# Routing moved from behind the last sum into it: pages opened tile by tile, rows scattered at once

## The chip, the cores and the metric

The kernel runs on one core of one Trainium2 chip. The time is the device time of that core in microseconds (us), the median of several runs. The profile is one further execution with the hardware profiler.

## The reference

Four graph layers over 3125 nodes of 256 features and 50000 edges, each added to its input and layer-normalised. The last one holds the part that matters here, a top-2 mixture of experts:

```python
x = gc + (feats @ W_res + b_res)
logits = x @ Wg + bg                      # 64 experts
vals, idx = jax.lax.top_k(logits, 2)
gates = jax.nn.softmax(vals, axis=-1)
order = jnp.argsort(e_flat)               # rows grouped by expert, at most 1024 each
h1 = gelu(einsum('ecd,edh->ech', buf, w1) + b1);  h2 = einsum('ech,ehd->ecd', h1, w2) + b2
out = zeros.at[tok_s].add(g_s[:, None] * y_s)
y = x + out;  batch norm over the nodes
```

What counts is that each node's row goes to its two experts and comes back; in which place of an expert's buffer a row stands doesn't matter.

## The kernel before

The 3125 rows are T = 25 tiles of 128. The sum over edges is made as a product with a dense 3200 x 3200 matrix of edge counts, built in the first stages and kept in DRAM; it is applied seven times (stages l0, l1, h1a, h1b, h2a, h2b, l3). In each, TensorE goes through 25 tiles; a tile's sum is 25 matmuls of 128x512 (line 1044), its matrix block loaded by SyncE. Between these matmuls `aggregate` puts side steps for earlier tiles, every fourth matmul (`gap`), in the order of its list. Every engine has its own stream of instructions, in an order written out by `pipeline`: in turn n a stage with lag g works on tile n - g, and an engine takes its stages strictly in the order of the list. Semaphores join the engines. `Steps.done` makes the next instruction wait for the one before.

In l3 the side steps are: transpose of Xn (lag 1, line 1082, needs POOL's `l3_own`, line 1750), transpose of the sum G (lag 1), transpose of V (lag 2), the two dense products (lag 1), the logits (lag 2, line 1098). VectorE: `l3_sum` (lag 1, line 1494), `l3_x4` (lag 2, line 1631), `l3_top` (lag 3: bias, maximum, index, two copies, lines 1636 to 1642). POOL: `l3_own` copies the tile's own rows to Xn (lag 1), `l3_keep` copies V to X4 (lag 2, line 1755).

Behind l3 comes the stage "route". VectorE (`dve_moe`) makes one-hot rows for all tiles at once, a running count over the tiles (line 600), and TensorE ranks the rows (lines 482 to 485). From the counts come each expert's pages of 128 rows, in the experts' order (lines 605 to 614), the table `etab` of the expert of each page, and each row's slot (lines 627 to 641). SyncE then loads the weights of the first four pages (lines 421, 425); POOL scatters the rows in 50 indirect DMAs of 128 rows (line 731) into `expert_rows_in` and waits for them. All engines meet at `phase_end`.

In the stage "experts" each page takes a turn: SyncE loads rows, w1, w2 and b2 (a ring of four), TensorE transposes the rows (line 494) and makes both products (lines 502, 512), POOL stores the result (line 741). In "combine" POOL gathers each row's two results (line 750), VectorE weighs and adds them and normalises.

## Time and profile before

| | |
|---|---|
| median of 3 runs | 2228.75 us (2226.08 to 2236.04) |
| profiled execution | 2222.63 us, its span 2221.0 us |
| TensorE (PE) busy | 1861.6 us, 84% |
| VectorE (DVE) busy | 829.7 us, 37% |
| ScalarE (ACT) busy | 469.3 us, 21% |
| GpSimd (POOL) busy | 348.8 us, 16% |
| stage l3 | about 1414 to 1636 us |
| stage route | 1636 to 1736 us |
| stage experts | 1736 to about 2071 us |

The times of the rows count from the span's start. A busy time is the sum of an engine's instructions; a row of the timeline has in brackets the engine's idle time before it and what ended that. PE is a matmul, PEld the load of its weights, SPq a DMA issued by SyncE. The granted clock is TensorE's, as a share of 2.4 GHz.

### The profile page before, as it was taken

To read this page: it belongs to the slowest core of one execution; us is meant where nothing else is said; L and a number is where in the kernel's file an instruction comes from. 1 tells how busy PE (TensorE), PEld (TensorE's weight loads), DVE (VectorE), ACT (ScalarE), POOL (GpSimd) and SP (SyncE) were. 2 spreads that over 40 slices of the span, in tenths; PEclk is the share of its full clock that TensorE was granted. 3 is DMA by queue.
4 is the path that set the end of the run, shared out by engine and by line. 5 is a ranking of instruction groups with operands and counts; after the bars stand their busy time and mean duration, and the time that the engine had idled before them with its cause. 6 is when DMAs were issued, how large, how long until landed. Compare 5 with 4: busy or idle time off the path is not lost. (4 is left out here: it accounts for less than half of the span.)

```text
span 2221.0 us, 32876 instructions
## 1 busy us (share of the span) xinstructions
PE 1861.6 (84%) x9113; PEld 1473.7 (66%) x9115; DVE 829.7 (37%) x2415; ACT 469.3 (21%) x1245; POOL 348.8 (16%) x573
## 2 busy tenths in 40 slices
PE   1888989799899899999999999899940699999441
PEld 0355656588688688777778788688830688888320
DVE  4865554444434411122211177412151122222256
ACT  0033344322223211111111111111110223223010
POOL 1011222311111100000000022100007111111361
PEclk8566555899999999999999999999975799999656
DMA  4167888999688688766678888788823699999521
GB/s 118 30 237 260 279 290 301 341 319 320 214 278 265 196 272 290 251 214 213 216 240 286 277 288 290 250 289 275 279 67 125 214 368 373 372 373 374 186 78 58
DMA packets 284883, 553.32 MB, mean 249 GB/s; under 512 B 17170, under 2 KB 208328, under 8 KB 281608
## 3 DMA queue, kind: packets, MB, share of 16 engines
q1 hardware_dynamic: 275976, 528.36, 71.2%
q0 software_dynamic: 8832, 24.13, 3.2%
q8 instruction: 27, 0.44, 0.1%
q14 instruction: 48, 0.39, 0.1%
HBM read 415.14 MB, written 137.29 MB: 249 GB/s over the span
## 5 line engine op out<-in xcount | busy, mean ns | idle before, releaser
L1044 PE MATMUL psum<-xsa,blk 128*128 128x512 f32 x2500 | 637.6, 405 | 14.6 <-DVEq L342 8.2
L1044 PEld LDWEIGHTS psum<-xsa,blk 128*128 128x128 f32 x2500 | 463.8, 191 | 107.0 <-DVEq L342 8.7
L1044 PE MATMUL psum<-xsb,blk 128*128 128x512 f32 (+1 forms) x1875 | 416.6, 369 | 5.9 <-DVEq L342 5.9
L1044 PEld LDWEIGHTS psum<-xsb,blk 128*128 128x128 f32 x1875 | 322.2, 190 | 64.4 <-issue 7.2
L1386 DVE TENSOR_SCALAR onehots<-counts_scratch 128x348 bf16<-128x348 f16 x464 | 161.5, 374 | 119.3 <-PE psum L949 75.1
L949 PE MATMUL psum<-onehots 128*128 128x349 bf16 x464 | 166.8, 466 | 40.9 <-DVE onehots L1391 39.7
L502 PE MATMUL psum<-route,expert_weights 128*128 128x128 f32 x1360 | 169.8, 279 | 0.0
L502 PEld LDWEIGHTS psum<-route,expert_weights 128*128 128x128 f32 x1360 | 160.3, 194 | 1.2
L512 PE MATMUL psum<-expert_weights,route 128*128 128x256 f32 x672 | 159.1, 380 | 0.2 <-ACT route L561 0.2
L949 PEld LDWEIGHTS psum<-onehots 128*128 128x128 bf16 x464 | 51.9, 112 | 146.5 <-DVE onehots L1386 116.1
L1730 POOL TENSOR_SCALAR ve<-mv 128x1 f32<-128x1 f32 x75 | 16.8, 223 | 822.2 <-DVE mv L1501 822.2
L561 ACT ACTIVATE route<-psum,b1T 128x128 f32<-128x128 f32 x340 | 96.9, 368 | 229.1 <-PE psum L502 229.1
L968 PE MATMUL psum<-identR,band_rows 128*128 128x130 f32 x625 | 139.3, 405 | 6.1 <-ACT blk L1163 5.3
L968 PEld LDWEIGHTS psum<-identR,band_rows 128*128 128x128 f32 x625 | 132.2, 319 | 9.8 <-ACT blk L1163 5.5
L669 DVE TENSOR_TENSOR route<-psum,route 128x256 f32<-128x256 f32 x84 | 35.7, 425 | 257.9 <-PE psum L512 257.9
L512 PEld LDWEIGHTS psum<-expert_weights,route 128*128 128x128 f32 x672 | 121.3, 190 | 13.4 <-ACT route L561 0.4
L494 PE MATMUL psum<-identF,route 128*128 128x128 f32 x172 | 35.7, 290 | 86.8 <-DMA route<-expert_rows_in 86.3
L1494 DVE SCALAR_TENSOR_TENSOR G<-psum,binv,Lo 128x256 f32<-128x256 f32 x50 | 24.2, 484 | 219.8 <-ACT Lo L1215 219.8
L1222 ACT ACTIVATE tT<-psum 128x256 f32<-128x256 f32 x175 | 67.1, 384 | 171.7 <-PE psum L1082 170.2
L741 POOL DMA_DIRECT2D expert_rows_out<-route x84 | 45.4, 541 | 298.4 <-DVE route L669 298.4
L494 PEld LDWEIGHTS psum<-identF,route 128*128 128x128 f32 x172 | 18.3, 143 | 110.0 <-DMA route<-expert_rows_in 92.5
L1494 DVE SCALAR_TENSOR_TENSOR G<-psum,ndst,Lo 128x256 f32<-128x256 f32 x50 | 24.2, 484 | 179.0 <-ACT Lo L1215 176.7
(292 smaller groups left out, 1859.5 us busy)
## 6 DMA issues: line engine op xcount, KB each, us to landing
blk<-counts_src_on_rows SPq DMA_DIRECT2D x125, 832.0 KB, 4.6
blk<-counts_src_on_rows SPq DMA_DIRECT2D x125, 768.0 KB, 4.4
expert_weights<-in_L_gnn_w SPq DMA_DIRECT2D x176, 512.0 KB, 6.2
blk<-counts_dst_on_rows SPq DMA_DIRECT2D x50, 832.0 KB, 4.5
counts_dst_on_rows<-band_rows SPq DMA_DIRECT2D x25, 1600.0 KB, 7.2
blk<-counts_dst_on_rows SPq DMA_DIRECT2D x50, 768.0 KB, 4.3
counts_src_on_rows<-blk SPq DMA_DIRECT2D x13, 1600.0 KB, 8.1
counts_src_on_rows<-rblk SPq DMA_DIRECT2D x12, 1600.0 KB, 8.6
```

The source lines that it names most:

```text
L494: mm = e.transpose(psum[:, par, k * P:(k + 1) * P], xin[n][:, k * P:(k + 1) * P], identF[:, :])
L502: mm = e.matmul(psum[:, 2 + par, h * P:(h + 1) * P], w1s[n][:, k, h * P:(h + 1) * P], xTs[par][:, k * P:(k + 1) * P], start=(k == 0), stop ...
L512: mm = e.matmul(psum[:, 4 + par, 0:F], hTs[par][:, h, :], w2s[n][:, h, :], start=(h == 0), stop=(h == HT - 1))
L561: mm = e.activation(hTs[par][:, h, :], psum[:, 2 + par, h * P:(h + 1) * P], ACT.Gelu, bias=b1T[:, h, bass.ds(ex, 1)])
L669: e.tensor_tensor(yout[n], psum[:, 4 + par, 0:F], b2s[n], ALU.add)\
L741: e.dma_start(ybuf[bass.ds(c * P, P), :], yout[n]).then_inc(S(f"rows_stored{n}"), 16)
L949: e.matmul(o, one_d[:, u, :], one_s[:, u, 0:FW + 1], start=False, stop=True, skip_group_check=True).then_inc(S("onehots_used"), 1)
L968: mm = e.matmul(psum[:, s + k // 3, o:o + TURNED], band_rows[par][:, t * P:(t + 1) * P], identR[:, :], start=True, stop=True)
L1044: mm = e.matmul(o, blk[n][:, k * P:(k + 1) * P], XS[:, k, :, 0:Fw], start=(k == 0), stop=(k == T - 1 and not own))
L1222: e.activation(o, pick(a, par), func, **kw).then_inc(S("tile_" + sig), 1)
L1386: e.tensor_scalar(one_s[:, u, 0:FW], iota_f, scol[:, bass.ds(c, 1)], wcol[:, bass.ds(c, 1)], ALU.is_equal, ALU.mult).then_inc(S("sources_r ...
L1494: e.scalar_tensor_tensor((G if o is None else o)[:, 0:w], agg[par][:, 0:w], tcol(scale, i), Lo[:, 0:w], ALU.mult, ALU.add).then_inc(S("til ...
```

## The change

The route stage's work is put into l3, tile by tile. `l3_top` also makes the tile's one-hot rows `picks` and their sum `chosen`. TensorE has a new side step, `ranks` (lag 4, third in the list): two matmuls give each row's rank within the tile and the tile's count for each expert. VectorE has a new stage `l3_slots` (lag 4), which keeps for each expert the room left in its open page, the place where that ends, and the number of pages opened; where a tile's rows pass the room, it opens the next free page. From this come the slots of the tile's rows (`slot_to`, line 1656 of the changed kernel). POOL has a new stage `l3_scatter` (lag 4): it waits for the slots, issues the tile's two scatters (line 1782), and adds the opened pages to `page_expert` (line 1786). Its own copy is now line 1770 and keep line 1775. Pages thus stand in the order in which they are opened, not in the experts' order; `dve_moe` only makes the table from `page_expert`. The deepest lag of l3 is 4 instead of 2 on TensorE and 3 on VectorE. Both logits buffers become one (`logits_read`), since bank 7 of PSUM holds the ranks.

```diff
@@ -473,17 +483,6 @@
...
-            e.wait_ge(S("running_counts"), 1)
-            tpb = BANK // NE
...
-            e.matmul(psum[:, 4, 0:NE], onesB[:, :], before_tile[:, T, :], start=True, stop=True)\
-                .then_inc(S("ranked"), 1)
...
@@ -583,64 +582,19 @@
         def dve_moe(e):
             phase_end(e, "l3")
             st = Steps(e, S("dve_route"))
-            e.tensor_tensor(gap, top_val[:, :, 1], top_val[:, :, 0], ALU.subtract).then_inc(S("top_gap"), 1)
-            st.done(e.tensor_copy(idxf, top_idx[:, :, 0:TOP]))
-            one_hot = (OH1, OH2)
...
-            st.done(e.tensor_tensor(chosen, OH1, OH2, ALU.add))
...
-            for t in range(T):
-                st.done(e.tensor_tensor(before_tile[:, t + 1, :], before_tile[:, t, :], chosen[:, t, :], ALU.add))
-            e.sem_inc(S("running_counts"), 1)
-            e.wait_ge(S("ranked"), 1)
...
+            e.wait_ge(S("pages_noted"), T)
+            st.done(e.tensor_tensor(page_expert, page_expert, iota_e[:, :], ALU.mult))
+            e.tensor_reduce(ecol[:, 0:1], page_expert, AX.X, ALU.add).then_inc(S("chunk_experts"), 1)
+            st.done(e.tensor_scalar(eint[0:1, 0:1], pages[0:1, 0:1], float(RING - 1), None, ALU.add))
             st.done(e.tensor_scalar(nturn[0:1, 0:1], eint[0:1, 0:1], RING.bit_length() - 1, None,
...
             e.wait_ge(S("chunk_experts_up"), 1)
             st.done(e.tensor_copy(etab[0:1, :], psum[0:1, 6, 0:P]))
             e.sem_inc(S("experts_known"), 1)
-            first_row = ebase.unsqueeze(1).to_broadcast([P, T, NE])
-            for k in range(TOP):
-                st.done(e.tensor_tensor(M, one_hot[k], ranks, ALU.mult))
...
-                st.done(e.scalar_tensor_tensor(keep[:, k, :], rk[:, k, :], float(CAP), valid[:, :],
-                                               ALU.is_lt, ALU.mult))
-                st.done(e.tensor_tensor(slot[:, k, :], slot[:, k, :], keep[:, k, :], ALU.mult))
-                st.done(e.tensor_copy(slot_from[:, k, :], slot[:, k, :]))
-                st.done(e.tensor_scalar(rk[:, k, :], keep[:, k, :], -1.0, 1.0, ALU.mult, ALU.add))
-                st.done(e.tensor_tensor(rk[:, k, :], rk[:, k, :], trash[:, k, :], ALU.mult))
-                st.done(e.tensor_tensor(slot[:, k, :], slot[:, k, :], rk[:, k, :], ALU.add))
-                st.done(e.tensor_copy(slot_to[:, k, :], slot[:, k, :]))
-                e.sem_inc(S("slots_ready"), 1)
+            e.tensor_tensor(gap, top_val[:, :, 1], top_val[:, :, 0], ALU.subtract).then_inc(S("top_gap"), 1)
+            st.done(e.tensor_scalar(keep, slot, 0.0, None, ALU.is_ge))
+            st.done(e.tensor_scalar(slot_from[:, :, :], slot, 0.0, None, ALU.max))
...
@@ -724,12 +678,6 @@
         def pool_moe(e):
             phase_end(e, "l3")
-            for k in range(TOP):
-                e.wait_ge(S("slots_ready"), k + 1)
-                for t in range(T):
-                    e.indirect_dma_start(out=xbuf, out_offset=bass.IndirectOffsetOnAxis(ap=slot_to[:, k, t:t + 1], axis=0),
-                                         in_=X4[:, t, :], in_offset=None).then_inc(S("rows_scattered"), 16)
...
@@ -1094,6 +1042,8 @@
+                    if sig == "logits" and not (isinstance(i, int) and i == 0):
+                        e.wait_ge(S("logits_read"), i)
@@ -1101,6 +1051,14 @@
...
+            def ranks(i, par):
+                e.wait_ge(S("picks_made"), i + 1)
+                e.wait_ge(S("ranks_read"), i + 1)
+                e.matmul(psum[:, 7, 0:NE], triB[:, :], chosen[par], start=True, stop=True)
+                e.matmul(psum[:, 7, NE:2 * NE], onesB[:, :], chosen[par], start=True, stop=True)\
+                    .then_inc(S("picks_ranked"), 1)
...
@@ -1123,9 +1081,10 @@
             aggregate("l3", XSa, F, False, [
                 (1, turn("l3", "own_copied", "x_turned", pT2, Xn, KF)),
                 (1, turn("l3", "sum_read", "g_turned", pT, G, KF)),
+                (4, ranks),
                 (2, turn("l3", "x4_made", "x4_turned", px4, V, KF)),
                 (1, dense("l3", ["xT", "gT"], "pre", pD[0], two(tT, wgc) + two(tT2, wrs))),
-                (2, dense("l3", ["x4T"], "logits", [o[:, 0:NE] for o in pD2], two(tT3, wgt)))])
+                (2, dense("l3", ["x4T"], "logits", pD2[0][:, 0:NE], two(tT3, wgt)))])
...
@@ -1619,7 +1578,17 @@
...
-            st4 = Steps(e, S("steps_l3"), 3)
+            st4 = Steps(e, S("steps_l3"), 4)
+            e.memset(rooms[:, 0, :], 0.0)
+            e.memset(rooms[:, 1, :], float(CAP))
+            e.memset(ends_at, 0.0)
+            e.memset(pages, 0.0)
+            st.done(e.memset(page_expert, 0.0))
+            st.done(e.tensor_scalar(page_first, pcol[:, 0:1], float(P), None, ALU.mult))
+            st.done(e.tensor_scalar(beyond, valid[:, T - 1:T], -1.0, FALL, ALU.add, ALU.mult))
+            e.sem_inc(S("pages_set"), 1)
+            e.sem_inc(S("ranks_read"), 1)
...
@@ -1632,16 +1601,67 @@
             def l3_top(i, par):
                 st4.tile(i)
+                if i >= 2:
+                    e.wait_ge(S("picks_ranked"), i - 1)
                 e.wait_ge(S("tile_logits"), past("l3", "logits") + i + 1)
-                st4.done(e.tensor_tensor(U[:, 0:NE], pD2[par][:, 0:NE], bgb[:, :], ALU.add))
+                e.tensor_tensor(U[:, 0:NE], pD2[0][:, 0:NE], bgb[:, :], ALU.add).then_inc(S("logits_read"), 1)
+                e.wait_ge(S("logits_read"), i + 1)
...
                 e.tensor_copy(row(top_val, i), max8[:, 0:TOP])
-                e.tensor_copy(row(top_idx, i), idx8[:, 0:TOP]).then_inc(S("tile_top"), 1)
-                e.wait_ge(S("tile_top"), past("l3", "top") + i + 1)
-            pipeline(e, [(1, l3_sum), (2, l3_x4), (3, l3_top)], unrolled=True)
+                st4.done(e.tensor_copy(top_idx[:, 0:TOP], idx8[:, 0:TOP]))
+                st4.done(e.tensor_tensor(picks[par], iota_e[:, :].unsqueeze(1).to_broadcast([P, TOP, NE]),
+                                         top_idx[:, 0:TOP].unsqueeze(2).to_broadcast([P, TOP, NE]), ALU.is_equal))
+                if i == T - 1:
+                    e.tensor_scalar(picks[par], picks[par], valid[:, T - 1:T], None, ALU.mult).then_inc(S("picks_valid"), 1)
+                    e.wait_ge(S("picks_valid"), 1)
+                e.tensor_tensor(chosen[par], picks[par][:, 0, :], picks[par][:, 1, :], ALU.add).then_inc(S("picks_made"), 1)
+            room, left = rooms[:, 0, :], rooms[:, 1, :]
+            st5 = Steps(e, S("steps_pages"), 19)
+            def l3_slots(i, par):
+                st5.tile(i)
+                e.wait_ge(S("picks_ranked"), i + 1)
+                if i >= 2:
+                    e.wait_ge(S("pages_noted"), i - 1)
+                rank, many = psum[:, 7, 0:NE], psum[:, 7, NE:2 * NE]
+                pair = [P, TOP, NE]
+                st5.done(e.tensor_tensor(taken, many, left, ALU.min))
+                st5.done(e.tensor_tensor(past_room, rank.unsqueeze(1).to_broadcast(pair), rooms, ALU.is_ge))
+                e.tensor_tensor(rows_of, rank, room, ALU.subtract).then_inc(S("ranks_read"), 1)
+                st5.done(e.tensor_tensor(new, taken, room, ALU.is_gt))
+                st5.done(e.tensor_tensor_scan(so_far, ones[:, 0:NE], new, 0.0, ALU.mult, ALU.add))
+                st5.done(e.tensor_tensor(first, so_far, new, ALU.subtract))
+                st5.done(e.tensor_scalar(first, first, pages[:, 0:1], float(P), ALU.add, ALU.mult))
+                st5.done(e.tensor_tensor(further, first, ends_at, ALU.subtract))
+                st5.done(e.tensor_tensor(past_room[:, 0, :], past_room[:, 0, :], further, ALU.mult))
+                e.wait_ge(S("ranks_read"), i + 2)
+                st5.done(e.tensor_tensor(rows_of, rows_of, ends_at, ALU.add))
+                st5.done(e.tensor_tensor(rows_of, rows_of, past_room[:, 0, :], ALU.add))
+                st5.done(e.scalar_tensor_tensor(rows_of, past_room[:, 1, :], -FALL, rows_of, ALU.mult, ALU.add))
+                st5.done(e.tensor_tensor(picked, picks[par], rows_of.unsqueeze(1).to_broadcast(pair), ALU.mult))
+                st5.done(e.tensor_reduce(slot[:, :, i], picked, AX.X, ALU.add))
+                if i == T - 1:
+                    e.tensor_scalar(slot[:, :, i], slot[:, :, i], beyond, None, ALU.add).then_inc(S("picks_valid"), 1)
+                    e.wait_ge(S("picks_valid"), 2)
+                st5.done(e.scalar_tensor_tensor(above, slot[:, :, i], 0.0, trash[:, :, i], ALU.is_lt, ALU.mult))
+                e.tensor_tensor(slot_to[:, :, i], slot[:, :, i], above, ALU.max).then_inc(S("slots_ready"), 1)
+                st5.done(e.scalar_tensor_tensor(further, further, float(P), new, ALU.add, ALU.mult))
+                st5.done(e.tensor_tensor(ends_at, ends_at, further, ALU.add))
+                st5.done(e.tensor_tensor(rooms, rooms, taken.unsqueeze(1).to_broadcast(pair), ALU.subtract))
+                st5.done(e.scalar_tensor_tensor(room, new, float(P), room, ALU.mult, ALU.add))
+                e.scalar_tensor_tensor(of_page[par], first, page_first, new, ALU.is_equal, ALU.mult)                    .then_inc(S("pages_opened"), 1)
+                st5.done(e.tensor_tensor(pages, pages, so_far[:, NE - 1:NE], ALU.add))
+                e.wait_ge(S("slots_ready"), i + 1)
+            pipeline(e, [(1, l3_sum), (2, l3_x4), (3, l3_top), (4, l3_slots)], unrolled=True)
...
@@ -1754,7 +1774,19 @@
...
-            pipeline(e, [(1, l3_own), (2, l3_keep)], unrolled=True)
+            def l3_scatter(i, par):
+                e.wait_ge(S("slots_ready"), i + 1)
+                e.wait_ge(S("tile_x4_kept"), past("l3", "x4_kept") + i + 1)
+                for k in range(TOP):
+                    e.indirect_dma_start(out=xbuf, out_offset=bass.IndirectOffsetOnAxis(ap=slot_to[:, k, i:i + 1], axis=0),
+                                         in_=X4[:, i, :], in_offset=None).then_inc(S("rows_scattered"), 16)
+                e.wait_ge(S("pages_opened"), i + 1)
+                e.tensor_tensor(page_expert, page_expert, of_page[par], ALU.add).then_inc(S("pages_noted"), 1)
+                e.wait_ge(S("pages_noted"), i + 1)
+            e.wait_ge(S("pages_set"), 1)
+            pipeline(e, [(1, l3_own), (2, l3_keep), (4, l3_scatter)], unrolled=True)
...
```

On TensorE, one turn of l3's loop, before. `identF,Xn` and `identF,G` are the transposes of lag 1, `identF,V` that of lag 2:

```order
L1082 MATMUL psum<-identF,Xn 128x128 [waits tile_own_copied]
L1082 MATMUL psum<-identF,Xn 128x128
L1044 MATMUL psum<-xsa,blk 128x512 x4
L1079 REGISTER_ALU
L1082 MATMUL psum<-identF,G 128x128 [waits tile_sum_read]
L1082 MATMUL psum<-identF,G 128x128
L1044 MATMUL psum<-xsa,blk 128x512 x4
L1082 MATMUL psum<-identF,V 128x128 [waits tile_x4_made]
```

and in the changed kernel:

```order
L1030 MATMUL psum<-identF,Xn 128x128 [waits tile_own_copied]
L1030 MATMUL psum<-identF,Xn 128x128
L992 MATMUL psum<-xsa,blk 128x512 x4
L1030 MATMUL psum<-identF,G 128x128 [waits tile_sum_read]
L1030 MATMUL psum<-identF,G 128x128
L992 MATMUL psum<-xsa,blk 128x512 x4
L1059 MATMUL psum<-route,triB 128x64 [waits ranks_read,picks_made]
L1060 MATMUL psum<-route,onesB 128x64
L992 MATMUL psum<-xsa,blk 128x512
L992 MATMUL psum<-xsa,blk 128x512 [waits block_in01]
L992 MATMUL psum<-xsa,blk 128x512 x2
L1030 MATMUL psum<-identF,V 128x128 [waits tile_x4_made]
```

The ranks stand behind the two transposes of lag 1, and what came there before is four matmuls later.

On POOL, two turns of l3 before:

```order
L1750 COPY Xn<-X 128x256 [waits tile_x_turned]
L1755 COPY X<-V 128x256 [waits tile_x4_made]
L1750 COPY Xn<-X 128x256 [waits tile_x_turned]
L1755 COPY X<-V 128x256 [waits tile_x4_made]
L1750 COPY Xn<-X 128x256 [waits tile_x_turned]
```

and one in the changed kernel, with the copies on either side:

```order
L1775 COPY X<-V 128x256 [waits tile_x4_made]
L1782 DMA expert_rows_in<-X,slot_to 21248x256 [waits tile_x4_kept,slots_ready]
L1782 DMA expert_rows_in<-X,slot_to 21248x256
L1786 TENSOR_TENSOR route<-route 128x64 [waits pages_opened]
L1770 COPY Xn<-X 128x256 [waits tile_x_turned,pages_noted]
L1775 COPY X<-V 128x256 [waits tile_x4_made]
```

The scatters and the note stand between one tile's keep and the next tile's own copy.

## Rows read from the trace of the kernel before

**Rows 1.** Windows by stage (busy us, clock, DMA share, GB/s): l3, experts' stage.

```profile
core 0: us, PE busy (x) PEld busy (x) DVE busy (x) ACT busy (x) POOL busy (x), PEclk, DMA share, GB/s
...
1440.00:1628.00 188.00, 188.00 (x942) 156.95 (x941) 39.63 (x176) 35.37 (x87) 16.36 (x44) 1.00 0.77 258
...
1745.00:2080.00 335.00, 323.15 (x2172) 285.69 (x2171) 66.62 (x167) 96.56 (x340) 45.42 (x84) 0.99 1.04 361
```

**Rows 2.** Timeline (start us, duration us), PEld, one turn of l3.

```profile
1586.24 0.37 PEld L1082 LDWEIGHTS psum<-identF,Xn 128*128 128x128 f32 x2
...
1588.54 0.37 PEld L1082 LDWEIGHTS psum<-identF,V 128*128 128x128 f32 x2
...
1594.84 0.37 PEld L1082 LDWEIGHTS psum<-identF,Xn 128*128 128x128 f32 x2
```

**Rows 3.** Timeline of the same turn, VectorE and POOL.

```profile
1586.33 0.48 DVE L1494 SCALAR_TENSOR_TENSOR G<-psum,ndst,Lo 128x256 f32<-128x256 f32 x1 [6.44 <-ACT Lo L1215]
...
1586.85 0.42 DVE L1631 TENSOR_TENSOR V<-psum,bc_gc 128x256 f32<-128x256 f32 x1
...
1587.34 0.40 POOL L1755 COPY X<-V 128x256 f32<-128x256 f32 x1 [7.86 <-DVE V L1631]
...
1587.68 0.40 POOL L1750 COPY Xn<-X 128x256 f32<-128x256 f32 x1
...
1588.33 0.16 DVE L1642 COPY route<-idx 128x2 uint32<-128x2 uint32 x1
```

**Rows 4.** Timeline, VectorE's 64-column instructions behind l3.

```profile
1652.84 0.29 DVE L609 TENSOR_TENSOR_SCAN route<-ones,route 128x64 f32<-128x64 f32 x1
1653.16 0.23 DVE L610 TENSOR_TENSOR route<-route 128x64 f32<-128x64 f32 x1
1653.43 0.26 DVE L612 TENSOR_SCALAR route<-route,pcol 128x64 f32<-128x64 f32 x1
1653.72 0.22 DVE L613 TENSOR_REDUCE route<-route 128x1 f32<-128x64 f32 x1
1653.97 0.15 DVE L614 TENSOR_SCALAR route<-route 128x1 f32<-128x1 f32 x1
```

**Rows 5.** Timeline, from the last sum to the first expert matmul.

```profile
1628.78 0.47 ACT L1215 ACTIVATE Lo<-psum,ndst 128x256 f32<-128x256 f32 x1 [4.79 <-PE psum L1044]
...
1655.75 0.41 SPq L421 DMA_DIRECT2D expert_weights<-in_L_gnn_w  x1
...
1663.99 0.18 DVE L641 CAST slot_to<-route 128x25 uint32<-128x25 f32 x1
...
1665.21 1.26 POOL L731 DMA_INDIRECT expert_rows_in<-X,slot_to  x1 [31.35 <-DVEq L642]
...
1727.94 0.96 POOL L731 DMA_INDIRECT expert_rows_in<-X,slot_to  x1 [0.30 <-issue]
...
1736.52 0.69 PE L494 MATMUL psum<-identF,route 128*128 128x128 f32 x2 [82.06 <-DMA route<-expert_rows_in]
```

**Rows 6.** Windows as in rows 1, while the first weights load.

```profile
1667.00:1669.00 2.00, 0.00 (x0) 0.00 (x0) 1.97 (x2) 0.00 (x0) 1.70 (x2) 0.50 1.07 368
1669.00:1671.00 2.00, 0.00 (x0) 0.00 (x0) 1.97 (x2) 0.00 (x0) 1.43 (x2) 0.50 0.67 245
```

**Rows 7.** Timeline, TensorE's waits in h1b and at its end.

```profile
1090.72 0.44 PE L1082 MATMUL psum<-identF,G 128*128 128x128 f32 x2 [0.58 <-DVE G L1518]
...
1113.62 0.44 PE L1082 MATMUL psum<-identF,G 128*128 128x128 f32 x2 [2.40 <-DVE G L1518]
```

**Rows 8.** Windows as in rows 1, behind h1b's end.

```profile
1115.90:1119.30 3.40, 2.37 (x6) 1.96 (x7) 0.42 (x1) 0.18 (x1) 0.00 (x0) 0.51 0.00 0
```

**Rows 9.** Timeline, a gather beside a long add in the combine stage.

```profile
2100.74 1.48 DVE L683 TENSOR_TENSOR X<-X,bc_bet 128x1280 f32<-128x1280 f32 x1
2100.83 2.22 POOL L750 DMA_INDIRECT expert_weights<-expert_rows_out,slot_from  x1 [0.30 <-issue]
```

**Rows 10.** Line 750's gathers: ns min/median/max.

```profile
L750 POOL DMA_INDIRECT expert_weights<-expert_rows_out,slot_from x50: 942/946/2260, 2085.7 to 2152.3; - x50
```

69 lines of the change are left out of this document (24 added, 45 removed).

## Prediction

> **What bounds the kernel now.** I read the stage windows first [rows 1]. In l3, the last of the seven sums, TensorE is busy for all of the 188 us looked at, at full clock, and the DMA engines for 0.77; in the experts' stage it is busy for 323 of 335 us. So both are TensorE's. Between them lies a stretch in which TensorE does next to nothing, read from the timeline [rows 5]: the last tile's sum is being read at 1628.78, and the first expert matmul starts at 1736.52. Those 107.7 us are what the change is after. Most of them is POOL: 50 indirect scatters, the first at 1665.21, the last at 1727.94, thus 1.27 us apart, of which 0.96 is the instruction and 0.30 the step to the next.
>
> One turn of l3 is the other thing to see. TensorE's transpose of Xn starts at 1586.24 and the next turn's at 1594.84: a turn is 8.60 us [rows 2]. On DVE it holds 2.16 us of work (1586.33 to 1588.49), on POOL 0.74 us [rows 3]. All the rest of their time is free.
>
> **What goes.** The scatters between the stages, VectorE's 25 running counts and its 128x1600 passes over all tiles, and nine ranking matmuls. What is left between the last sum and the first expert matmul has to be built up anew.
>
> **What is added per turn.** *TensorE*: two bf16 matmuls of 64 columns (lines 1059 and 1060 of the changed kernel), with their loads. Two f32 loads for a transpose took 0.37 us [rows 2]; these are smaller and cost between nothing and that. I take 0.25, so TensorE's own turn becomes 8.85. *VectorE*: two more instructions in `l3_top` (0.5), and 22 in `l3_slots`. A dependent instruction of 64 columns follows the one before by 0.27, a scan by 0.32 and a reduction by 0.25 [rows 4]; for 128 columns I take 0.34, between 64 columns (0.23 long) and 256 (0.48 long) [rows 3, 4]. Up to `slot_to` there are sixteen: ten of 64 columns (one doesn't wait) 2.5, three of 128 columns 1.0, the scan 0.32, two of 2 columns 0.4: 4.2 us. The six behind it, which POOL's scatter doesn't need, cost 1.4. VectorE's turn is 2.16 + 0.5 + 5.6 = 8.3 us, just inside 8.85. Alone it would hide, with 0.5 us to spare. *POOL*: two scatters and a 128x64 add, some 3 us; alone it would hide as well. *DMA*: 256 KB more per turn, at a share of 0.77 [rows 1]; I cost it at nothing, hidden by the free share; without that cover it is 0.7 us a turn at the 361 GB/s of the experts' stage.
>
> **What they are worth in a ring.** They are not alone, since POOL takes its steps in one order: own copy, keep, then the wait for the slots, the scatters, the note. The next tile's own copy (Xn) is queued behind that wait, and TensorE's transpose waits for that copy, three matmuls into its turn. The slots wait for the ranks, which TensorE makes behind the two transposes of the same turn. So one turn's transpose depends on the last one's through three engines:
> - transpose of Xn to ranks made: from 1586.24 to 1588.54, where the transpose of V stands now, is 2.30 [rows 2]; with the ranks and the pipeline's end 2.85;
> - slots up to `slot_to`: 4.2, and 0.05 for the semaphore;
> - `slot_to` to the first scatter: 1664.17 to 1665.21 is 1.04, the semaphore's own instruction included [rows 5]. POOL's plain copy of V starts at 1587.34, 0.07 after the instruction that made V ends at 1587.27 [rows 3]. These are the two bounds; I take 0.9, since it is the same instruction;
> - two scatters, 0.96 + 0.30 + 0.96 [rows 5], with 0.1 for meeting VectorE: 2.3;
> - the add for the page's expert, between nothing and the 0.40 of a 256-column copy [rows 3], and a step to it and a wait for itself: 0.5;
> - the own copy 0.40 [rows 3] and the semaphores: 0.5.
>
> The sum is **11.3 us**, against a TensorE turn of 8.85: TensorE stands for 2.45 us in each turn ahead of its transpose. What is queued behind is the whole sum of that tile. The first scatter is in turn 4, so 20 turns grow by 11.3 - 8.6 = 2.7 us: **+54 us**. With every bound at its low end (0.07 for the start, nothing for the add) the ring is 10.1, with the high ones 11.6.
>
> **The clock in it.** In h1b TensorE waits 0.58 us in every turn and keeps full clock. At that stage's end it waited 2.40 us, and the next stage began at a granted 0.51, that is the 1.2 GHz level, for 3.4 us [rows 7, 8]. A wait of 2.45 in every turn is of the second kind. 3.4 us at half clock lose 1.7 us of matmul time, and as they begin near the end of the wait they fall upon the transposes and ranks, which are part of the ring. Bounds: nothing in any turn, or 1.7 in all 20, 34 us. I take 1.35 in two turns of three, about 0.9 on average: **+18 us**. The Trainium skill, "TensorE: Matmul & The Clock Gate", Part 1, says that "the default state is throttled, and activity releases the throttle"; by that a ring which leaves TensorE idle pays twice, and by the opposite view, a clock that only a long stop takes away, the sum below would be 18 us lower. The two rows of this trace lean to the first.
>
> **The tail.** From the last tile's sum (1628.78 now) the new order runs: VectorE starts 0.6 later, but the ranks it needs stand behind the own copy that still waits for POOL; slots of tile 21 from 4.0 to 9.7; then turns of 7.9 and 7.5 us to 25.1, as each still has tops and slots; the last `slot_to` at 29.8; scatters and note to 33.5. Nothing of this is under the sum, since the slots lag four tiles. Then 0.25 for the stage's end, two instructions on the page table, 0.5, and from the experts' column (ended at 1654.12) to SyncE's first weight load (1655.75) 1.63 as now [rows 4, 5]: 35.9. The 4 MB of the eight first loads kept the DMA engines full until about 1670, 14.3 us after that issue [rows 6]. These loads were covered by the scatters and now lie open: the first rows are issued behind them. With 0.6 for rows and start, the first expert matmul comes at **50.8 us** in place of 107.7: **-57 us**. The experts' stage then starts with the same full ring of weights, so I let it and everything behind it unchanged, the number of pages too: a page is opened when an expert's room is used up, as many as a count rounded up gives.
>
> **Sum.** -57 + 54 + 18 = +15 us, on the profiled execution's 2222.63: 2237.6. The median of the runs shown is 6.1 us over that execution, so I forecast **2244 us**, 0.7% slower. About 0.5%, 11 us, is what a measurement of this kernel tells from no change.
>
> **The rivals.**
> 1. *The ring holds, the clock doesn't fall.* For it: TensorE is still busy nearly 80% of a turn, far more than in the stretch behind the last sum. Against it: the row at h1b's end. Then -57 + 54 = -3 us: 2226, no change. Chance 0.25.
> 2. *Faster: the ring is shorter.* Its place is the start of the scatter behind its wait: the 1.04 us of the trace may be the cost of a queue that had been idle for 31 us. If POOL reaches the wait with the instruction prepared, and the add is cheap, the ring is 10.4 or less; TensorE then waits 1.5 us or less, the clock stays, and l3 gains 36 us: -21, 2208. The point that decides is a ring of 11.2 without clock loss, or about 10.8 with some. At its far end the ring falls under VectorE's 8.85 and the gain is -50. Chance 0.2, nearly all near -21.
> 3. *The ring is longer: POOL and VectorE hold each other up.* In the combine stage a scatter's sister, the gather of line 750, took 2.22 us in place of 0.95 beside VectorE's 1.48 us add of two SBUF operands [rows 9]. Here VectorE's two-operand instructions are 0.23 us each, and six to ten of them fall beside the scatters, the note and the own copy. If each of POOL's four waits out one or two, the ring is 12.3, and with the clock 13.5: -57 + 74 + 24 = +41, 2270. Against it: the 50 gathers have a median of 0.946 us [rows 10], though two instructions of 0.48 us run beside each pair. Chance 0.1. The Trainium skill, "SBUF — State Buffer", calls the pair of ports that VectorE and GpSimd share "an exclusive lock, not a bandwidth split", held for the whole of a VectorE instruction with two SBUF inputs against a GpSimd one that reads SBUF. By that rule this is the case to expect, though with short instructions a small one; the row of 2.22 agrees with it.
>
> **How the numbers follow.** The forecast case has 0.45: ring 11 to 11.6, clock lost in a part of the turns, +4 to +30 us. Slower by over 0.5%: most of that, 0.38, and rival 3: 0.48. Within 0.5%: rival 1 and the lower edge of the forecast: 0.27. Faster: rival 2 and what rival 1 gives below -11: 0.25. The likeliest case's own range is 2233 to 2259. The range is 2202 to 2276: down to rival 2 with a few us under it, up to rival 3; outside lies a ring that doesn't bind, and one over 12.5.
>
> **What will show it.** In the timeline of the changed l3 the transposes of Xn should stand 11 to 13 us apart from the fifth turn on and 8.6 before; TensorE's largest wait there should be on POOL's copy at line 1770, 2 us and more each, not on VectorE's sum. `slot_to` should be followed by the first scatter 0.9 us later. The granted clock of l3, now 1.00, should fall to 0.8 to 0.95. From the last sum to the first expert matmul should be 51 us, with the DMA engines full for about 14 of them and no POOL scatter behind the first 34. I am wrong if the turn stays under 10 us (the ring doesn't bind: some 50 us faster), if TensorE waits for VectorE instead (its turn is over 9), or if the tail is over 60 us.

## The result, and the profile after

| | before | changed |
|---|---|---|
| median, same chip | 2228.31 us (4 runs, 2226.08 to 2236.04) | 2202.60 us (4 runs, 2201.74 to 2204.00) |
| ratio, 95% interval | | 0.9888 [0.9871, 0.9906] |
| profiled execution | 2222.63 us, span 2221.0 | 2202.93 us, span 2201.2 |

The change makes the kernel 1.1% faster. The forecast was 0.7% slower, so the sign is wrong; 2202.6 lies at the very edge of the range. It is the case of rival 2: a ring shorter than 10.4 us, full clock. Between the profiled executions the change is 19.7 us, between the medians 25.7; the median before lies 5.7 us over its profiled execution, and the changed kernel's 0.3 under.

The windows of the changed kernel, as in [rows 1], for l3 ahead of the fourth turn, l3 with the scatters in it, the tail with its two halves, and the experts' stage:

```profile
core 0: us, PE busy (x) PEld busy (x) DVE busy (x) ACT busy (x) POOL busy (x), PEclk, DMA share, GB/s
1440.00:1455.00 15.00, 15.00 (x76) 12.21 (x76) 6.33 (x28) 3.26 (x8) 1.15 (x3) 1.00 0.83 271
1455.00:1640.00 185.00, 162.57 (x815) 128.16 (x815) 131.07 (x580) 29.30 (x72) 55.05 (x90) 1.00 0.82 261
1663.00:1700.00 37.00, 6.90 (x34) 5.14 (x34) 26.41 (x120) 1.79 (x5) 11.79 (x18) 0.60 0.10 36
1700.00:1718.00 18.00, 0.91 (x5) 0.50 (x5) 2.34 (x13) 0.49 (x2) 0.00 (x0) 0.50 0.84 277
1735.00:2050.00 315.00, 310.49 (x2100) 276.15 (x2100) 64.41 (x162) 91.70 (x321) 43.91 (x81) 1.00 1.07 369
```

TensorE was busy for 188.00 of 188.00 us of l3 before. Now it stands for 22.4 of 185, while its granted clock stays at 1.00. Who holds it is one row of TensorE's waits from 1440 to 1663 us (total us, times, longest):

```profile
PE psum L1030 <- POOL Xn L1770: 24.9, 20, 1.5
```

That is the own copy, in 20 turns, as the ring would have it, but 1.24 us each and not 2.45. One turn in the timeline, all engines:

```profile
1593.80 0.44 PE L1030 MATMUL psum<-identF,Xn 128*128 128x128 f32 x2 [1.24 <-POOL Xn L1770]
...
1596.43 0.22 DVE L1636 TENSOR_TENSOR route<-psum,route 128x64 f32<-128x64 f32 x1 [1.37 <-PE psum L1060]
...
1600.43 0.16 DVE L1656 TENSOR_TENSOR slot_to<-route 128x2 uint32<-128x2 f32 x1
...
1600.87 0.99 POOL L1782 DMA_INDIRECT expert_rows_in<-X,slot_to  x1 [6.78 <-DVE slot_to L1656]
...
1602.17 0.97 POOL L1782 DMA_INDIRECT expert_rows_in<-X,slot_to  x1 [0.30 <-issue]
...
1603.16 0.34 POOL L1786 TENSOR_TENSOR route<-route 128x64 f32<-128x64 f32 x1
1603.56 0.40 POOL L1770 COPY Xn<-X 128x256 f32<-128x256 f32 x1
...
1604.01 0.44 PE L1030 MATMUL psum<-identF,Xn 128*128 128x128 f32 x2 [1.23 <-POOL Xn L1770]
```

The ring can be read off it: 1593.80, 1596.43, 1600.59 (end of `slot_to`), 1600.87, 1603.16, 1604.01.

| part of the ring | forecast | measured |
|---|---|---|
| transpose of Xn to the ranks' reader | 2.90 | 2.63 |
| slots up to `slot_to` | 4.20 | 4.16 |
| `slot_to` to the first scatter | 0.90 | 0.28 |
| two scatters | 2.30 | 2.29 |
| note, own copy, semaphores | 1.00 | 0.85 |
| sum | 11.3 | 10.21 |

The tail, from the last tile's sum to the first expert matmul, which answers to [rows 5]:

```profile
1663.22 0.47 ACT L1174 ACTIVATE Lo<-psum,ndst 128x256 f32<-128x256 f32 x1 [3.86 <-PE psum L992]
...
1692.14 0.17 DVE L1656 TENSOR_TENSOR slot_to<-route 128x2 uint32<-128x2 f32 x1
...
1693.08 0.99 POOL L1782 DMA_INDIRECT expert_rows_in<-X,slot_to  x1 [3.44 <-issue]
...
1695.36 0.33 POOL L1786 TENSOR_TENSOR route<-route 128x64 f32<-128x64 f32 x1
1699.90 0.23 DVE L586 TENSOR_TENSOR route<-route,iota_e 128x64 f32<-128x64 f32 x1 [6.18 <-POOLq L352]
...
1702.17 0.41 SPq L431 DMA_DIRECT2D expert_weights<-in_L_gnn_w  x1
...
1718.50 1.39 PE L493 MATMUL psum<-identF,route 128*128 128x128 f32 x4 [17.59 <-DMA route<-expert_rows_in]
```

Where the 19.7 us between the profiled executions come from: l3 starts 1.9 us later (1416.35 for 1414.48); the last sum is read at 1663.22 in place of 1628.78, 34.4 later, so l3 itself is 32.6 longer (20 turns of 10.21 - 8.60 give 32.2); from there to the first expert matmul it is 55.3 us in place of 107.7, -52.5; the experts' stage gives 1.7. The 1.9 and the 1.7 say nothing of the change: over the kernels below that alter neither place, l3 starts at 1411.9 to 1417.3 us and the experts' stage takes 345.4 to 350.4. Two things in the tail were not in the forecast: 4.2 us between the end of the last note (1695.69) and the end of the stage, for which everybody waits for POOL's queue (L352 is `phase_end`); and the scatter at 1693.08 starts 0.77 us behind its `slot_to`, where it is 0.28 in the ring.

### The profile page after: what moved, and what is told of

Its sections match the earlier page's. It is cut to its first block and busy times, and to the rows that moved or that the text cites. A ratio compares the mean times of both kernels' runs of the same rounds, so it can differ in the third digit from the quotient of the medians.

```text
span 2201.2 us, 33702 instructions
## 1 busy us (share of the span) xinstructions
PE 1870.5 (85%) x9155; PEld 1472.8 (67%) x9156; DVE 936.2 (43%) x2962; ACT 469.5 (21%) x1245; POOL 360.6 (16%) x598
## 5 line engine op out<-in xcount | busy, mean ns | idle before, releaser
L916 PEld LDWEIGHTS psum<-identR,band_rows 128*128 128x128 f32 x625 | 132.1, 318 | 10.1 <-ACT blk L1122 5.8
L1782 POOL DMA_INDIRECT expert_rows_in<-X,slot_to x50 | 49.5, 990 | 168.2 <-DVE slot_to L1656 151.6
L1453 DVE SCALAR_TENSOR_TENSOR V<-psum,dinv,Lo 128x256 f32<-128x256 f32 x25 | 12.1, 484 | 140.8 <-ACT Lo L1174 140.8
L1725 POOL CAST band_rows<-digits 128x1044 fp32r<-128x1044 uint8 x50 | 56.3, 1153 | 91.1 <-DVE digits L1379 91.0
```

Source lines behind the costliest of these rows:

```text
L916: mm = e.matmul(psum[:, s + k // 3, o:o + TURNED], band_rows[par][:, t * P:(t + 1) * P], identR[:, :], start=True, stop=True)
L1453: e.scalar_tensor_tensor((G if o is None else o)[:, 0:w], agg[par][:, 0:w], tcol(scale, i), Lo[:, 0:w], ALU.mult, ALU.add).then_inc(S("til ...
L1725: e.tensor_copy(fields_of(band_rows[par], m), digit(m)).then_inc(S("lower_cast"), 1)
L1782: e.indirect_dma_start(out=xbuf, out_offset=bass.IndirectOffsetOnAxis(ap=slot_to[:, k, i:i + 1], axis=0), in_=X4[:, i, :], in_offset=None) ...
```

## The experiments

Eleven kernels. Each was timed beside the kernel before on its own chip; a ratio of 0.9888 is "like the changed kernel", and a hundredth is 22 us. Short diffs are against the changed kernel. "Over" and "under the changed kernel" are the difference of the ratios times 2226 us; each ratio has an interval of 3 to 8 us to either side.

**The ring taken away.** POOL copies the tile's own rows a turn ahead, so the copy TensorE waits for is no longer queued behind the same turn's scatter.

```diff
-            pipeline(e, [(1, l3_own), (2, l3_keep), (4, l3_scatter)], unrolled=True)
+            pipeline(e, [(0, l3_own), (2, l3_keep), (4, l3_scatter)], unrolled=True)
```

> The changed kernel with POOL's own copy one tile earlier (lag 0 for 1), so that the next transpose no longer waits for this turn's scatter. Theory (a ring TensorE, VectorE, POOL sets l3's turn): the ring is opened, the transposes of Xn stand 8.85 us apart in place of 10.22, TensorE no longer waits on POOL's copy, 20 turns save 27 us: about 2175 us. Rival (VectorE or the DMA traffic sets the turn and the copy is only the last to be seen): the turn stays above 9.8 us, TensorE waits for VectorE's sum or for a block, under 10 us saved.

Measured: 2172.85 us, ratio 0.9752 [0.9732, 0.9771], 30 us under the changed kernel. The transposes of Xn in TensorE's timeline wait for nothing (no bracket) and stand 8.78 apart:

```profile
1599.51 0.38 PE L1030 MATMUL psum<-identF,Xn 128*128 128x128 f32 x2
1608.28 0.38 PE L1030 MATMUL psum<-identF,Xn 128*128 128x128 f32 x2
1617.07 0.38 PE L1030 MATMUL psum<-identF,Xn 128*128 128x128 f32 x2
```

So the ring was the only thing that lengthened l3 beyond TensorE's own work, and one number in a list takes it out. The added matmuls cost 8.78 - 8.60 = 0.18 us a turn (0.25 forecast), VectorE's work, put at 8.3 us a turn, and POOL's fit beside them.

**The ring lengthened.** Three copies of 256 columns more, ahead of the own copy.

```diff
             def l3_own(i, par):
...
+                e.tensor_copy(R2[:, :], X[:, bass.ds(i, 1), :].rearrange("p a f -> p (a f)"))
+                e.tensor_copy(V2[:, :], X[:, bass.ds(i, 1), :].rearrange("p a f -> p (a f)"))
+                e.tensor_copy(G2[:, :], X[:, bass.ds(i, 1), :].rearrange("p a f -> p (a f)"))
```

> Three more copies of 256 columns on POOL ahead of the own copy, each about 0.35 us, nothing else: the ring grows from 10.2 to about 11.3 us, the length that the prediction gave it. Clock theory of the prediction: TensorE's wait grows to about 2.4 us, the granted clock of l3 falls below 0.95 and the turn is over 11.8 us, some +35 us against the changed kernel. Rival (the clock holds through such waits): clock 1.00, turn 11.3, +21 us.

Measured: 2235.08 us, ratio 1.0043 [1.0026, 1.0060], 34 over the changed kernel. TensorE's timeline, then two windows of l3 (columns as in the windows above):

```profile
1615.75 0.44 PE L1030 MATMUL psum<-identF,Xn 128*128 128x128 f32 x2 [1.55 <-POOL Xn L1773]
...
1626.99 0.44 PE L1030 MATMUL psum<-identF,Xn 128*128 128x128 f32 x2 [2.26 <-POOL Xn L1773]
...
1638.25 0.44 PE L1030 MATMUL psum<-identF,Xn 128*128 128x128 f32 x2 [2.26 <-POOL Xn L1773]
...
1650.75 0.44 PE L1030 MATMUL psum<-identF,Xn 128*128 128x128 f32 x2 [1.94 <-POOL Xn L1773]
```

```profile
1500.00:1550.00 50.00, 42.08 (x198) 32.76 (x197) 31.74 (x138) 6.88 (x17) 16.37 (x32) 0.94 0.74 229
1550.00:1600.00 50.00, 41.51 (x196) 32.52 (x194) 31.86 (x139) 6.50 (x16) 16.94 (x33) 0.93 0.72 228
```

Ten of the 20 turns are 11.25 us (as 1615.75 to 1626.99), the other ten 12.1 to 12.8 (as 1638.25 to 1650.75, 12.5); the windows' clock of 0.92 to 0.94 goes with them. Twenty turns of 11.25 - 10.21 are 21 us. The long turns are 11.5 us over that in all, by the starts of the transposes; what is left of the 34 us over the ring's 21 is 13. So the clock costs 11 to 13 us. This is the kernel that the prediction described, ring of 11.3 with waits of 2.3 us, where the forecast had 18 for its clock.

**Why 0.77 us at the last two tiles and 0.28 in the ring? Was it a third semaphore?** At the last two tiles the scatter waits for three semaphores and not two, as the wait for the last note comes in front. Here it has one more in every turn, behind the two, for an event long past (a passed wait).

```diff
                 e.wait_ge(S("slots_ready"), i + 1)
                 e.wait_ge(S("tile_x4_kept"), past("l3", "x4_kept") + i + 1)
+                e.wait_ge(S("tile_x4_made"), past("l3", "x4_made") + i + 1)
```

> The first scatter of each tile waits for one more semaphore, one that is always passed already. slot_to to scatter is 0.28 us in l3's turns (two semaphores) and 0.77 in the last turns (three). Theory (the third semaphore costs it): 0.77 in every turn, the ring 10.7, +10 us. Rival (it is the end of the stage, or what POOL did before, that costs it): 0.28 stays, no change.

Measured: 2200.75 us, ratio 0.9886 [0.9869, 0.9902]; `slot_to` 1609.58 to 1609.74, scatter at 1610.02: 0.28 still. A third wait by itself costs nothing.

**Or the note's wait ahead of the others,** as it stands at the last tiles?

```diff
+                if i >= 1:
+                    e.wait_ge(S("pages_noted"), i)
                 e.wait_ge(S("slots_ready"), i + 1)
```

> The changed kernel with one more wait ahead of each scatter, placed first: for the note of the tile before, which POOL has long finished. In the changed kernel's profile the scatter starts 0.28 us behind the slot_to it waits for in the ring, where the waits are slots_ready and tile_x4_kept, and 0.77 us behind it at the last two tiles, where nothing stands between note and scatter and the wait on the note is added in front. Theory: three waits with the note's in front cost the 0.77, wherever they stand. Then the scatter starts 0.77 behind slot_to in every turn, the ring grows by 0.49 to 10.7 us, and 20 turns cost 10 us: about 2212. Rival: the 0.77 has nothing to do with the wait (the instruction before, or an engine that sat idle); then 0.28 stays in the ring, turns stay 10.2 and the time 2202.

Measured: 2214.20 us, ratio 0.9951 [0.9934, 0.9967], 14 over the changed kernel. `slot_to` and scatter in the timeline:

```profile
1609.30 0.16 DVE L1656 TENSOR_TENSOR slot_to<-route 128x2 uint32<-128x2 f32 x1
...
1610.23 0.99 POOL L1784 DMA_INDIRECT expert_rows_in<-X,slot_to  x1 [7.27 <-issue]
```

0.76 to 0.78 in all 22 tiles from the second to the last but two: reproduced. The first, which has no such wait, has 0.31; the last two, which have it twice, 0.87 and 1.19. The ring is 10.7 and TensorE waits 1.7 us. Three turns of 12.28 now stand between (one from 1613.37 to 1625.65); windows put the granted clock from 1614.00 to 1617.00 at 0.50 to 0.52. So at 1.7 us the clock falls in some turns: 20 times 0.49 us and three times 1.6 make the 14 us.

**Or the separate increment of `slots_ready`,** which the kernel before had between `slot_to` and the scatter?

```diff
-                e.tensor_tensor(slot_to[:, :, i], slot[:, :, i], above, ALU.max).then_inc(S("slots_ready"), 1)
+                st5.done(e.tensor_tensor(slot_to[:, :, i], slot[:, :, i], above, ALU.max))
+                e.sem_inc(S("slots_ready"), 1)
...
```

> The changed kernel, but VectorE tells POOL of the slots as the kernel before did: it waits for slot_to's own semaphore and then adds to slots_ready by an instruction of its own, in place of slot_to's own increment. Theory: a good part of the 1.04 us that the prediction took as the start of a scatter was this separate instruction and the wait before it. Then slot_to to scatter grows from 0.28 to between 0.5 and 0.7 and the ring from 10.2 to about 10.5, 20 turns +6 us: 2208. If it is all of it (1.04), the ring is 11.0 and the time 2218 or more, as the clock begins to fall. Rival: it costs under 0.1 us, the start 0.28 to 0.35, the time 2202 to 2204; then the 1.04 was the first scatter's own, behind a long stop.

Measured: 2206.88 us (2198.27 to 2207.89), ratio 0.9917 [0.9898, 0.9936]. The time doesn't separate the two; the rows do: `slot_to` ends at 1607.29, the scatter starts at 1607.63, 0.34. The increment costs 0.06. The rival holds: the 1.04 of [rows 5] was mostly not the semaphore. The next run has more on it. The first scatter of all is also longer, 1.26 us here and before.

**The two waits the other way round.**

```diff
-                e.wait_ge(S("slots_ready"), i + 1)
                 e.wait_ge(S("tile_x4_kept"), past("l3", "x4_kept") + i + 1)
+                e.wait_ge(S("slots_ready"), i + 1)
```

> The changed kernel with the scatter's two waits in the other order: first tile_x4_kept, long passed, then slots_ready, which is the one that comes late. What the runs have shown: slots_ready first and one or two passed waits behind it, 0.28 us from slot_to to the scatter; a passed wait on pages_noted first and slots_ready second of three, 0.77. Theory: what counts is whether the late wait stands first. Then it is 0.77 here with two waits too, the ring is 10.7 us, and the time 13 us over the changed kernel's as with the extra wait: ratio 0.995. Rival: the order doesn't matter by itself, it takes the third wait with the note's in front (pages_noted is raised by POOL itself); then 0.28 stays, and the time is that of the changed kernel, ratio 0.989.

Measured: 2217.28 us, ratio 0.9969 [0.9953, 0.9985], 18 over the changed kernel. VectorE and POOL in the timeline:

```profile
1607.87 0.17 DVE L1656 TENSOR_TENSOR slot_to<-route 128x2 uint32<-128x2 f32 x1
...
1608.81 0.99 POOL L1782 DMA_INDIRECT expert_rows_in<-X,slot_to  x1 [7.29 <-DVE slot_to L1656]
```

0.77 to 0.81 from the second tile on, with two waits. What counts is whether the wait that ends late stands first. It does in the ring of the changed kernel (0.28) and with the third wait behind (0.28); it stands second here, with the note's wait, and at the last two tiles of the changed kernel, where the wait on the note is carried over into the scatter (0.77 each time). The swap of two lines costs 0.5 us a turn, 10 us in 20 turns. Two turns of 12.3 us among those of 10.7, where the windows' clock is 0.96 and 0.97 (1455 to 1550), cost 3 more. That makes 13 to 14 of the 18 us, and l3 is 13.5 us longer in this profile; the other 4 are within the intervals of the two ratios. With the lines this way round the change would have been 0.3% faster, which is no change by the measure of the forecast.

The first scatter of all tells what the 1.04 of [rows 5] was. Here, then in the changed kernel:

```profile
1454.09 0.16 DVE L1656 TENSOR_TENSOR slot_to<-route 128x2 uint32<-128x2 f32 x1
1455.23 1.26 POOL L1782 DMA_INDIRECT expert_rows_in<-X,slot_to  x1 [6.53 <-DVE slot_to L1656]
```

```profile
1457.12 0.16 DVE L1656 TENSOR_TENSOR slot_to<-route 128x2 uint32<-128x2 f32 x1
...
1457.59 1.26 POOL L1782 DMA_INDIRECT expert_rows_in<-X,slot_to  x1 [5.86 <-DVE slot_to L1656]
```

It starts 0.98 us behind `slot_to` with the passed wait in front, and 0.31 with the late wait in front. In the kernel before, the first scatter had the passed wait for the stage's end in front of that for `slots_ready`, and the separate increment: 0.98 + 0.06 is the 1.04. POOL had stood for 6.5 us here and for 31 there, so the long stop isn't needed to explain it. The kernel before with its waits exchanged was not run.

**The scatters behind l3.** Slots are still made tile by tile, the 50 scatters stand behind POOL's end of l3.

```diff
             phase_end(e, "l3")
+            for i in range(T):
+                for k in range(TOP):
+                    e.indirect_dma_start(out=xbuf, out_offset=bass.IndirectOffsetOnAxis(ap=slot_to[:, k, i:i + 1], axis=0),
+                                         in_=X4[:, i, :], in_offset=None).then_inc(S("rows_scattered"), 16)
...
```

(`l3_scatter` keeps only the note.)

> Slots in the sum as in the changed kernel, but all 50 scatters on POOL behind its l3 steps. Ring theory: without the scatters' 2.5 us the ring is 7.7 us, under TensorE's turn of 8.85, so l3 is 27 us shorter; the scatters, 63.5 us from the last sum on, end 33 us later than now, of which the drain of 4 us is saved and the weights' loads (16 us from issue to rows) are hidden again: first expert matmul about 70 us behind the last sum in place of 55. Together about -12 us against the changed kernel, 2190. Rival (hiding the scatters is what the change gains): slower than the changed kernel by 15 us or more.

Measured: 2227.77 us, ratio 1.0011 [1.0000, 1.0023], 27 over the changed kernel, and not the 2190 of the theory: the rival came. The scatters start only when the last slots are made and the stage is over, 31.5 us behind the last sum, and TensorE waits for rows. POOL's last note and first scatter, then TensorE:

```profile
1669.27 0.32 POOL L1784 TENSOR_TENSOR route<-route 128x64 f32<-128x64 f32 x1 [5.52 <-DVE route L1665]
1670.62 1.26 POOL L683 DMA_INDIRECT expert_rows_in<-X,slot_to  x1 [1.03 <-POOLq L352]
```

```profile
1741.50 0.69 PE L493 MATMUL psum<-identF,route 128*128 128x128 f32 x2 [70.79 <-DMA route<-expert_rows_in]
```

l3's turn is 9.0 us without the scatters in it (PE's transposes at 1603.95, 1612.96), which is 1.2 under the ring. But the stretch of 63 us of scatters is open again, and the first expert matmul comes 102.4 us behind the last sum, where the expectation had 70. The first scatter, with a single wait, starts 0.9 us after the stage's end (1669.70 to 1670.62), so a stage's end right ahead of a first scatter costs about as much as a passed wait does. Making slots early is worth nothing unless the scatters go early too.

**POOL's end of l3 without the drain.**

```diff
-            phase_end(e, "l3")
+            phase_end(e, "l3", drained=False)
```

(with `drained=False` it is `e.sem_inc(S("phases_ended"), 1)` in place of `e.drain().then_inc(...)`)

> The changed kernel, but POOL reports the end of l3 by an increment of the semaphore and not by a drain; the wait for all scattered rows, which stands at the end of the route stage, is kept. Theory: the 4.2 us between the last note (1695.69) and the end of the stage (1699.90) are the drain waiting until the scatters' data has landed. Then VectorE's page table starts 4 us sooner, SyncE's first weight load comes about 29 + 3.4 + 2.5 = 35 us behind the last sum in place of 39, and the time is 4 us less: 2198.5. Rival: what takes 4.2 us is the scatters' own queue or another engine's end of stage; then the wait moves and the time is the same, 2202.

Measured: 2199.48 us, ratio 0.9879 [0.9859, 0.9898], 2 us under the changed kernel. The time alone doesn't show 4 us, the timeline does. POOL's note, SyncE's first weights, the first expert matmul:

```profile
1694.87 0.33 POOL L1789 TENSOR_TENSOR route<-route 128x64 f32<-128x64 f32 x1
...
1697.57 0.41 SPq L434 DMA_DIRECT2D expert_weights<-in_L_gnn_w  x1
...
1712.60 1.43 PE L496 MATMUL psum<-identF,route 128*128 128x128 f32 x4 [16.29 <-DMA route<-expert_rows_in]
```

From note's end to weights it is 2.4 us in place of 6.5. So the 4.2 us are the drain's. They need scatters ahead of it: in the run before this one, where POOL's l3 has none, the last note ends at 1669.59 and the other engines are released at 1669.70, 0.1 us later, drain included. What the drain waits for is not shown. Not for the data alone: the changed kernel's last scatter is issued at 1694.37, its DMA engines move nothing from 1696.50 on, and the stage ends at 1699.90. The Trainium skill, "DMA: Bandwidth & Descriptors", in "Anatomy of one DMA — SWDGE (gpsimd) path", lays most of a DMA's fixed cost of about 2 us on the receipt of its last byte, and says it may be long where the target is HBM. The trace has 2.4 us from issue to landing for these last two scatters; that ends at about 1696.8, 1.1 us behind the note, and 3.1 of the 4.2 us stay open.

**Fewer weights ahead of the rows.** SyncE loads the first page's w1 and w2 before the end of the route stage, the others behind their page's rows.

```diff
-            for c in range(RING):
+            for c in range(1):
                 ex = expert_of(c)
                 load_w1(ex, c)
                 load_w2(ex, c)
             phase_end(e, "route")
             for c in range(RING):
                 load_rows(c, c)
+                if c >= 1:
...
```

> The changed kernel, but SyncE loads only the first page's w1 and w2 (1 MB of 4) before the end of the route stage; the other three pages' weights are issued each behind that page's rows. In the changed kernel all 4 MB are ahead of the first rows, and TensorE's first expert matmul comes 16.3 us after the first weight load. Theory: this wait is the queue of the weights; with 1 MB ahead the matmul comes 6 to 8 us after that load, 9 us sooner, and the first experts then meet weights that are late: of the 9 us between 3 and 9 stay, 2194 to 2199. Rival: the stage's first pages are bound by the load of their weights whichever comes first (0.5 MB a matrix, 369 GB/s, 2.8 us for each page's two against a page's 13 us), so that nothing is given back: all 9 us stay, 2193. Other rival: rows landing behind the scatters bound the start; then the first matmul moves by less than 3 us and the time stays 2202.

Measured: 2190.78 us, ratio 0.9853 [0.9817, 0.9889], 8 under the changed kernel. SyncE's first weights, rows and TensorE's first matmul:

```profile
1701.98 0.41 SPq L431 DMA_DIRECT2D expert_weights<-in_L_gnn_w  x1
1703.15 0.35 SPq L428 DMA_DIRECT2D route<-expert_rows_in  x1
...
1707.64 0.69 PE L497 MATMUL psum<-identF,route 128*128 128x128 f32 x2 [6.91 <-DMA route<-expert_rows_in]
```

5.7 us from the first weights in place of 16.3. The experts' stage takes 347.4 us to the combine's first matmul (2055.08), and 346.7 in the changed kernel (2065.21): under 1 us is given back, by these two profiles. That is the first rival's case and not the theory's; the runs are spread over 13 us (2188.25 to 2201.75), so the 8 us are loosely known.

**Together.**

> Two of the three edits: POOL copies the tile's own rows a turn ahead, and its l3 ends without the drain. Theory: as above, 30 + 2 to 4 us: 2169 to 2171, ratio 0.974. Rival: in this order the scatters' data has landed by the time VectorE is done with its last tile, and the drain no longer costs anything: 2172.9, as with the first edit alone.

Measured: 2171.86 us, ratio 0.9737 [0.9723, 0.9752]. By the profile the drain costs the same here: from note's end to first weights 2.4 us, and 6.5 with the drain. By the time the difference from the 0.9752 of the first edit alone is within the intervals.

> Three edits together: POOL copies the tile's own rows in the turn before they are used (so they no longer stand behind the scatter), l3's end on POOL without the drain, and the first page's weights alone ahead of the rows. Measured alone against the kernel before of the same chip: 0.9752 for the first, 0.9879 and 0.9853 for the others, where the changed kernel has 0.9888. If the savings add up (30, 2 and 8 us): 2202.6 - 40 = 2162, ratio 0.971. Theory: the three stand in different places (ring, stage's end, first load) and do add up: 2160 to 2166. Rival: with the ring gone the first weight load is waited for by something else, and one of the two small savings is lost: 2168 to 2173.

Measured: 2166.20 us (5 runs, 2162.60 to 2172.31), ratio 0.9716 [0.9698, 0.9735]: 2.8% under the kernel before, and 38 us under the changed kernel, of 40 expected. By the medians the three savings add up, but the third's part is not shown: the intervals of the last two ratios overlap, and in the profile of this kernel the experts' stage takes 356.9 us, 11.2 over that of the kernel without the third edit, more than the 9.5 us by which the first expert matmul comes sooner behind the last sum. TensorE waits there for rows 18 times more after the first page, 13 us in all. One profile each doesn't tell how often that happens.

## Why the prediction was wrong

**What bounds, and what the change does: right.** The path was the ring through three engines that the prediction wrote down, with TensorE waiting on line 1770 in 20 turns. The experiment that cut the ring gave back 30 us. TensorE's own turn (8.78 for 8.85) and VectorE's slots (4.16 for 4.2) were as worked out.

**The failed step is the start of the scatter behind its wait.** The prediction had two rows, 0.07 of a copy and 1.04 of the first scatter of the kernel before, and took 0.9 "since it is the same instruction". It is 0.28. The instruction was the same, but its surroundings weren't: it was the first scatter of all, with a passed wait ahead of the late one, which costs 0.98 where the late wait first costs 0.31, and with a separate increment of the semaphore, 0.06. The 49 behind it could not tell anything, as none of them waited. This one term is 0.62 of the 1.1 us by which the ring was too long; the transposes and ranks gave 0.27, the note and the copy 0.15. The measured ring stands near the prediction's own low end, 10.1.

**The clock followed from it.** The term of 18 us failed by its input, the wait. At waits of 2.26 us the clock does fall, to 0.93 on average, in ten of 20 turns, and costs 11 to 13 us (18 forecast, for two turns in three); at 1.7 it falls in two or three turns of 20; at the 1.24 us that the real ring leaves it stays at 1.00. The reading it came from was also short: the 3.4 us of [rows 8] are the length of that row's window and not of the low clock, since the trace has 0.50 for the next 3.4 us too (1119.30 to 1122.70), and the 2.40 us were not the only stand there, with 0.47 and 1.27 behind it. That the loss in a long turn, 1.15 us on average, came near the 1.35 is partly luck. What the Trainium skill ("TensorE: Matmul & The Clock Gate", Part 1) says of a throttled default state, named in the prediction, is seen in the longer rings and not in this one. Two terms hang on one number here: 0.6 us of ring are 12 us by themselves and, by the run with the note's wait (ring 10.7, clock 5 us), most of the clock's 18.

**With the ring right, the sum is right.** -57 + 32 + 0 = -25 us, and the tail's miss of 4.5 makes it -20.5, for -19.7 measured. Of the forecast's +54 the ring took 32, of +18 none. The sum was also right the other way: the kernel whose ring is 11.25 us came to a ratio of 1.0043 [1.0026, 1.0060], where the forecast was 0.7% slower. The 6.1 us that the forecast put on top, for the median over the profiled execution, didn't come again either.

**The tail: 55.3 us for 50.8.** The last `slot_to` 29.1 us behind the last sum (29.8), the end of the note 32.5 (33.5), SyncE's first weights 2.3 behind the stage's end (2.1), the first matmul 16.3 behind those (14.9). The stage's end itself, costed at 0.25 us, was 4.2: the drain of a queue that has just issued scatters. In the kernel before there were none ahead of that drain.

**The rivals.** Rival 2 came (2208 forecast), and it named the right place: "the 1.04 us of the trace may be the cost of a queue that had been idle". It had a chance of 0.2, too little for a term whose two bounds, 0.07 and 1.04, both rested on one instruction of another kind or place. The long stop that it names need not be the cause, as the runs give 0.98 and 0.06 without it. Its point of decision is also worked out wrongly: a ring of 11.2 without clock loss gives -57 + 52 = -5 us, still no change; the -11 is reached at 10.9. Rival 3, the hold-ups of POOL and VectorE, did not show. The 50 scatters of line 1782 (min/median/max in ns):

```profile
L1782 POOL DMA_INDIRECT expert_rows_in<-X,slot_to x50: 963/985/1263, 1457.6 to 1694.4; - x50
```

All but the first are 0.96 to 1.00 in the timeline, at most 0.04 us over the 0.96 of [rows 5]. The hold-up of [rows 9] was beside a VectorE instruction of 1.48 us. Beside ones of 0.23 us no more than these 0.04 us are seen, so the exclusive lock of the Trainium skill ("SBUF — State Buffer", "SBUF: two separate sides"), which the prediction cited, makes next to no difference here. Length isn't all of it: in the kernel before, of two scatters beside one product of 1.87 us (line 629) one took 1.43 us and the other 0.96.

**Nothing given back later: right.** The experts' stage is 1.7 us shorter, within what it varies by, and not longer, and DMA's share of 0.82 in l3 held nobody up; with the ring cut it runs at 0.91 and TensorE is still busy all the time.

## What to carry to other kernels

When one engine's steps run in one order, look for the step whose result the matrix engine needs soonest, and put it ahead of the waits and not behind them: here one lag in a list is worth 30 us. A stage boundary exposes whatever used to hide in the stretch removed, so list what stands in the queues there (a drain behind scatters, 3 MB of weights that nobody needs yet): 4 us in the timeline for the one, 8 in the time for the other where it stood alone. And where a sum turns on one row that was read once, in a place unlike the new one, give the other value more than one chance in five.

## What the runs showed that was not expected

- **The order of two waits.** An indirect DMA on POOL starts 0.28 us behind the event when the wait for that event stands first, and 0.77 when it stands behind a wait long passed. The changed kernel, the third wait, the note's wait and the swap agree; why is not known, and for other instructions it was not tried. For the first scatter of all it is 0.31 and 0.98. With the late wait second, the kernel is 18 us slower, of which the ring's 0.5 us a turn and the clock explain 13 to 14.
- **The clock's dependence on a short wait.** One wait in a turn of l3: 1.24 us in 10.2, clock 1.00; 1.7 in 10.7, two or three slow turns of 20 and windows of 0.96 to 1.00; 2.26 in 11.25, ten of 20 and 0.92 to 0.94.
- **The drain.** 4.2 us on POOL behind two indirect scatters and a note, 0.1 us behind a note alone; 3.1 of the 4.2 lie behind the scatters' landing.
